# Ternary feed-forward layer: the value half and the product move to VectorE, both rounding passes to ScalarE, and the tile loop is written out

## The reference, cut to what matters

```python
def bit_linear(x, w, b):
    gamma_x = clip(max(abs(x), axis=-1, keepdims=True), 1e-05, None)
    scale_x = 127.0 / gamma_x
    x_dq = clip(round(x * scale_x), -128.0, 127.0) / scale_x
    gamma_w = clip(mean(abs(w)), 1e-05, None)
    w_dq = clip(round(w / gamma_w), -1.0, 1.0) * gamma_w
    return einsum('bsd,hd->bsh', x_dq, w_dq) + b
gate = silu(bit_linear(x, gate_w, gate_b))      # 256 -> 1024
val = bit_linear(x, val_w, val_b)               # 256 -> 1024
return bit_linear(gate * val, out_w, out_b)     # 1024 -> 256, added to x
```

## Time and profile before

| | |
|---|---|
| median of 3 runs | 2538.33 us (2534.33 to 2542.36) |
| the profiled execution's own time | 2534.81 us |
| its span in the profile | 2533.1 us |
| busy: TensorE matmul, VectorE, ScalarE, GpSimd | 1971.6, 1433.2, 1018.5, 822.2 us |
| the stage of the change | first VectorE instruction at 2383.33 us, last at 2529.58 us |
| granted TensorE clock, mean of the execution | 0.884 |

### The profile page before, as it was taken

The page is one execution under the profiler, slowest core; times in us unless marked ns, Lnnn a source line. Parts: engine busy times, 40 slices in busy tenths (PEclk is TensorE's granted clock), DMA queues, the critical chain, the costliest instruction groups (busy, mean ns, idle before and its releaser), DMA issues. The chain is left out here.

```text
span 2533.1 us, 45181 instructions
## 1 busy us (share of the span) xinstructions
PE 1971.6 (78%) x12069; PEld 1342.1 (53%) x12070; DVE 1433.2 (57%) x3465; ACT 1018.5 (40%) x2717; POOL 822.2 (32%) x783
## 2 busy tenths in 40 slices
PE   4999999979998997245599997388755689898355
PEld 3666666655555655123466665255523457676122
DVE  3565666647763335135533443677678517777598
ACT  3454455542222121012244443155477326767233
POOL 1333333320000001661255655122100126655276
PEclk9999999999998898677799999599967889989576
DMA  9940000000000002222487885200010011111000
GB/s 307 283 115 0 0 0 0 0 1 0 0 0 1 0 0 95 102 96 83 111 165 167 174 167 81 67 1 0 0 52 1 4 26 30 35 34 32 22 15 19
DMA packets 143984, 144.79 MB, mean 57 GB/s; under 512 B 49216, under 2 KB 133408, under 8 KB 143136
## 3 DMA queue, kind: packets, MB, share of 16 engines
q1 hardware_dynamic: 120864, 113.81, 15.6%
q0 software_dynamic: 23040, 30.01, 7.1%
HBM read 137.12 MB, written 66.44 MB: 80 GB/s over the span
## 5 line engine op out<-in xcount | busy, mean ns | idle before, releaser
L1406 POOL DMA_INDIRECT expert_sums<-moe_rows_in,moe_to x128 | 197.9, 1546 | 228.3 <-ACT moe_rows_in L1598 133.6
L1492 PE MATMUL moe_gate<-moe_places,moe_xt 128*128 x512 | 175.9, 466 | 2.0 <-issue 1.2
L1681 DVE COPY moe_ht_e<-moe_turned 128x256 f32<-128x256 f32 x128 | 54.3, 424 | 197.9 <-PE moe_turned L1500 171.1
L2723 POOL TENSOR_TENSOR wa_low<-wa_low,wa_top 128x512 f32<-128x512 f32 x128 | 133.1, 1040 | 101.7 <-DVE wa_top L2924 100.8
L251 POOL TENSOR_TENSOR ga_q_inv<-ga_q_sum,half 128x4 f32<-128x4 f32 x64 | 64.4, 1007 | 312.4 <-DVE ga_q_sum L421 312.4
L529 ACT ACTIVATE ga_prob<-ga_score,ga_neg_max 128x128 f32<-128x128 f32 x256 | 99.6, 390 | 153.9 <-DVE ga_neg_max L438 153.9
L2921 DVE SCALAR_TENSOR_TENSOR wa_low<-wa_score,wa_table 128x512 f32<-128x512 f32 x128 | 87.8, 686 | 63.1 <-PE wa_score L2762 60.6
L347 PE MATMUL ga_summed<-ga_wo,ga_out_t 128*128 128x256 f32 x512 | 122.8, 383 | 0.7 <-ACT ga_out_t L537 0.7
L285 PE MATMUL ga_proj<-ga_wq,ga_xt 128*128 128x512 f32 x256 | 122.6, 602 | 0.0
L347 PEld LDWEIGHTS ga_summed<-ga_wo,ga_out_t 128*128 128x128 f32 x512 | 98.1, 192 | 40.6 <-issue 29.2
L1189 POOL DMA_INDIRECT slot_x<-moe_xn,mr_slot_to x96 | 94.5, 985 | 70.4 <-issue 51.9
(11 more groups left out here) (430 smaller groups left out, 5113.2 us busy)
## 6 DMA issues: line engine op xcount, KB each, us to landing
moe_places<-in_L_ffn_packed SPq DMA_DIRECT2D x128, 608.0 KB
slot_x<-zeros SPq DMA_DIRECT2D x24, 1076.0 KB, 16.2
moe_rows_in<-slot_x SPq DMA_DIRECT2D x128, 134.5 KB
mc_rows<-expert_sums SPq DMA_DIRECT2D x8, 512.0 KB, 7.6
wa_v<-v_ctx SPq DMA_DIRECT2D x16, 180.0 KB, 3.0
x<-in_x SPq DMA_DIRECT2D x1, 2048.0 KB, 8.7
ctxt<-in_ctx_t SPq DMA_DIRECT2D x1, 2048.0 KB, 13.2
ga_wq<-in_L_xattn_Wq SPq DMA_DIRECT2D x1, 2048.0 KB, 16.9
```

The costliest lines, as they stand in the source:

```text
L1406: pool.indirect_dma_start(out=mem.sums[j % SUMS], out_offset=bass.IndirectOffsetOnAxis(ap=to[:, j:j + 1], axis=0), in_=y[:, j, :], in_offs ...
L1492: last = pe.matmul(both[j % 2][:, 0:2 * FE], xt[:, j % 2, c, :], packed[:, place, c * 2 * FE:(c + 1) * 2 * FE].rearrange("p a n -> p (a n) ...
L2723: pool.tensor_tensor(unit, unit, top[:, k % LOWS, :].unsqueeze(2).to_broadcast([P, QUAD, P]), ALU.subtract).then_inc(lowered.sem, 1)
```

## The change

Of the tile's work, the value half becomes one VectorE pass per half that reads PSUM, scales and adds the bias (L3186 of the changed kernel, the same form as `pre`). The product becomes a VectorE pass of 1024 columns (L3202), with two SBUF inputs. Both rounding passes become ScalarE `Identity` activations of 1024 columns: `shifted` with `per` as scale and a column of ROUND as bias (L3154), `rounded` with a column of -ROUND as bias (L3157); GpSimd fills the two columns once. ScalarE no longer moves the value banks. GpSimd keeps only the 16 additions of the output bias, issued one after another at the start of the stage. The copy into `xs` is gone; TensorE reads `mem.xnt16` itself. `gate`, `val` and `prod` have one buffer each; `far`, `size`, `per` and `scale_o` have two columns. Gate and value matmuls go gate, gate, value, value by halves with a signal for each half, and run one tile ahead and not two. All 16 tiles are written out, with constants for the tile numbers.

The diff, cut to its core:

```diff
         scale_g, scale_v = sb("scale_g", [P, B]), sb("scale_v", [P, B])
-        xs = sb("xs", [P, 2, HC, P], BF16)
-        pre, shifted = sb("pre", [P, F]), sb("shifted", [P, F])
-        gate, val = sb("gate", [P, 2, F]), sb("val", [P, 2, F])
+        pre, gate, val, prod, shifted = (sb(x, [P, F]) for x in ("pre", "gate", "val", "prod", "shifted"))
         rounded = sb("rounded", [P, F], BF16)
         ht = sb("ht", [P, FC, P], BF16)
...
+        up_by, down_by = sb("up_by", [P, 1]), sb("down_by", [P, 1])
+        far, size, per, scale_o = (sb(x, [P, 2]) for x in ("far", "size", "per", "scale_o"))
         gates = [bank(f"gates{j}") for j in range(2)]
         vals = [bank(f"vals{j}") for j in range(2)]
         turned, down = bank("turned", BF16), bank("down")
...
+        scaled, rounding_set = signal("scaled"), signal("rounding_set")
         biased = signal("biased")
-        multiplied = signal("multiplied", 1, 2)
...
+        gated, valued = signal("gated"), signal("valued")
+        pre_made, val_made, silued, multiplied = signal("pre"), signal("val"), signal("silued"), signal("multiplied")
+        chain, per_made = signal("chain"), signal("per")
+        lifted, rounded_s = signal("lifted"), signal("rounded")
+        turn, moved, downed, added = signal("turn"), signal("moved"), signal("downed"), signal("added")
+        def behind(engine, sig, n):
+            if n >= 0:
+                engine.wait_ge(sig.sem, sig.at(n))
...
         with nc.Block() as block:
             @block.gpsimd
             def _(pool):
...
+                pool.memset(up_by[:, :], ROUND).then_inc(rounding_set.sem, 1)
+                pool.memset(down_by[:, :], -ROUND).then_inc(rounding_set.sem, 1)
                 pool.wait_ge(mem.tf_loaded.sem, 16 * mem.tf_loads)
...
-                        pool.tensor_copy(xs[:, j % 2, :, :], mem.xnt16[:, :, bass.ds(n * P, P)]).then_inc(staged.sem, 1)
...
-                        pool.tensor_tensor(val[:, j % 2, :], val[:, j % 2, :], w.bv[:, :], ALU.add).then_inc(val_biased.sem, 1)
...
-                        pool.tensor_tensor(val[:, j % 2, :], val[:, j % 2, :], gate[:, j % 2, :], ALU.mult).then_inc(prod_made.sem, 1)
...
-                    pool.tensor_tensor(mem.x_tile(n), mem.x_tile(n), w.bo[:, :], ALU.add).then_inc(biased.sem, 1)
...
+                for n in range(B):
+                    pool.tensor_tensor(mem.x[:, n, :], mem.x[:, n, :], w.bo[:, :], ALU.add).then_inc(biased.sem, 1)
...
             @block.tensor
             def _(pe):
...
+                def up(n, out_banks, weight, read, done):
                     for h in range(2):
...
+                        behind(pe, read, 2 * (n - 1) + h)
+                        for c in range(HC):
+                            last = pe.matmul(out_banks[h][:, :], mem.xnt16[:, c, n * P:(n + 1) * P], weight[:, c, h * HALF:(h + 1) * HALF], start=(c == 0), stop=(c == HC - 1))
+                        last.then_inc(done.sem, 1)
+                def turn_product(n):
+                    pe.wait_ge(rounded_s.sem, rounded_s.at(n))
+                    behind(pe, moved, n - 1)
                     for f in range(FC):
                         last = pe.transpose(turned[:, f * P:(f + 1) * P], rounded[:, f * P:(f + 1) * P], mem.ident16[:, :])
                     last.then_inc(turn.sem, 1)
+                def go_down(n):
                     pe.wait_ge(moved.sem, moved.at(n))
...
+                    behind(pe, added, n - 1)
                     for f in range(FC):
                         last = pe.matmul(down[:, 0:H], ht[:, f, :], w.o[:, f, :], start=(f == 0), stop=(f == FC - 1))
                     last.then_inc(downed.sem, 1)
...
+                up(0, gates, w.g, pre_made, gated)
+                up(0, vals, w.v, val_made, valued)
+                for n in range(B):
+                    if n + 1 < B:
+                        up(n + 1, gates, w.g, pre_made, gated)
+                        up(n + 1, vals, w.v, val_made, valued)
+                    turn_product(n)
+                    go_down(n)
...
             @block.scalar
             def _(act):
...
+                def silu(n):
+                    behind(act, multiplied, n - 1)
                     for h in range(2):
-                        act.activation(val[:, j % 2, h * HALF:(h + 1) * HALF], vals[h][:, :], ACT.Copy, scale=scale_v[:, bass.ds(n, 1)]).then_inc(val_moved.sem, 1)
...
-                        act.activation(gate[:, j % 2, h * HALF:(h + 1) * HALF], pre[:, h * HALF:(h + 1) * HALF], ACT.Silu).then_inc(silued.sem, 1)
...
+                        act.wait_ge(pre_made.sem, pre_made.at(2 * n + h))
+                        act.activation(gate[:, h * HALF:(h + 1) * HALF], pre[:, h * HALF:(h + 1) * HALF], ACT.Silu).then_inc(silued.sem, 1)
+                def round_product(n):
+                    act.wait_ge(per_made.sem, per_made.at(n))
+                    act.activation(shifted[:, :], prod[:, :], ACT.Identity, bias=up_by[:, 0:1], scale=per[:, n % 2:n % 2 + 1]).then_inc(lifted.sem, 1)
+                    behind(act, turn, n - 1)
+                    act.wait_ge(lifted.sem, lifted.at(n))
+                    act.activation(rounded[:, :], shifted[:, :], ACT.Identity, bias=down_by[:, 0:1]).then_inc(rounded_s.sem, 1)
+                def move(n):
                     act.wait_ge(turn.sem, turn.at(n))
...
+                    behind(act, downed, n - 1)
                     act.activation(ht[:, :, :].rearrange("p c s -> p (c s)"), turned[:, :], ACT.Copy).then_inc(moved.sem, 1)
...
+                act.wait_ge(rounding_set.sem, 2)
+                silu(0)
+                for n in range(B):
+                    if n >= 1:
+                        move(n - 1)
+                    round_product(n)
+                    if n + 1 < B:
+                        silu(n + 1)
+                move(B - 1)
...
             @block.vector
             def _(dve):
                 dve.wait_ge(mem.tf_loaded.sem, 16 * mem.tf_loads)
...
                 dve.tensor_scalar(scale_g[:, :], mem.x_step[:, :], w.mean_g[:, 0:1], None, ALU.mult).then_inc(scaled.sem, 1)
                 dve.tensor_scalar(scale_v[:, :], mem.x_step[:, :], w.mean_v[:, 0:1], None, ALU.mult).then_inc(scaled.sem, 1)
                 dve.wait_ge(scaled.sem, 2)
...
+                def halves(n, target, banks, scale, bias, made, done, read):
                     for h in range(2):
                         cols = slice(h * HALF, (h + 1) * HALF)
...
+                        dve.wait_ge(made.sem, made.at(2 * n + h))
+                        behind(dve, *read(n, h))
+                        dve.scalar_tensor_tensor(target[:, cols], banks[h][:, :], scale[:, n:n + 1], bias[:, cols], ALU.mult, ALU.add).then_inc(done.sem, 1)
+                def before_silu(n):
+                    halves(n, pre, gates, scale_g, w.bg, gated, pre_made, lambda n, h: (silued, 2 * (n - 1) + h))
+                    halves(n, val, vals, scale_v, w.bv, valued, val_made, lambda n, h: (multiplied, n - 1))
+                def measure(n):
+                    j = slice(n % 2, n % 2 + 1)
                     def step(k, ins):
                         ins.then_inc(chain.sem, 1)
...
-                    step(2, dve.reciprocal(per[:, :], size[:, :]))
...
-                    step(3, dve.tensor_scalar(shifted[:, :], prod, per[:, 0:1], ROUND, ALU.mult, ALU.add))
...
-                    step(4, dve.tensor_scalar(rounded[:, :], shifted[:, :], ROUND, None, ALU.subtract))
+                        dve.wait_ge(chain.sem, chain.at(2 * n + k))
+                    dve.wait_ge(silued.sem, silued.at(2 * n + 1))
+                    dve.wait_ge(val_made.sem, val_made.at(2 * n + 1))
+                    behind(dve, lifted, n - 1)
+                    dve.tensor_tensor(prod[:, :], val[:, :], gate[:, :], ALU.mult).then_inc(multiplied.sem, 1)
+                    dve.wait_ge(multiplied.sem, multiplied.at(n))
+                    step(0, dve.tensor_reduce(far[:, j], prod[:, :], AX.X, ALU.max, apply_absolute_value=True))
+                    behind(dve, added, n - 2)
+                    step(1, dve.tensor_scalar(size[:, j], far[:, j], 1e-5, 1.0 / 127.0, ALU.max, ALU.mult))
+                    dve.reciprocal(per[:, j], size[:, j]).then_inc(per_made.sem, 1)
+                    dve.tensor_scalar(scale_o[:, j], size[:, j], w.mean_o[:, 0:1], None, ALU.mult).then_inc(scaled.sem, 1)
...
                 def finish(n):
...
-                    dve.tensor_scalar(scale_o[:, :], size[:, :], w.mean_o[:, 0:1], None, ALU.mult).then_inc(chain.sem, 1)
...
+                    row = mem.x[:, n, :]
+                    dve.wait_ge(scaled.sem, scaled.at(n + 2))
+                    dve.wait_ge(biased.sem, biased.at(n))
+                    dve.wait_ge(downed.sem, downed.at(n))
+                    dve.scalar_tensor_tensor(row, down[:, 0:H], scale_o[:, n % 2:n % 2 + 1], row, ALU.mult, ALU.add).then_inc(added.sem, 1)
...
                 before_silu(0)
...
+                for n in range(B):
```

(77 more changed lines are left out.)

54 lines of the change are left out of this document (2 added, 52 removed).

## The result

| | before | changed |
|---|---|---|
| median | 2536.33 us (4 runs) | 2503.74 us (2499.36 to 2516.61, 4 runs) |
| the profiled execution's own time | 2534.81 us | 2499.36 us |
| last stage, first VectorE instruction to the end of the last | 146.7 us | 115.9 us |
| start of the last stage | 2383.33 us | 2378.73 us |

The ratio is 0.9877, interval 0.9834 to 0.9919: the change saves about 31 us, and the interval leaves room for 20 to 42. The stage alone is 30.8 us shorter. The two profiled executions are 35.5 apart because the second also happened to enter the stage 4.6 us earlier, in code that is the same in both; medians of this kernel carry such scatter, the stage does not. Two further profiles of the changed kernel gave 116.0 and 115.9 us for the stage.

A forecast was written before the change was run, and what follows sets the result against it. VectorE, waiting for GpSimd, bounds the last stage; after the change start to 2391.1, 15 tiles of 6.7 and a last tile of 7.1 end at 2498.7 us, a 31.4 us gain, forecast 2507 us, range 2496 to 2520.

The forecast's parts named there:

- its two rounding passes mostly wait for GpSimd's instruction: VectorE, last stage before the change: `shifted` and `rounded` take 4.23 us a tile, 1.44 when left alone.
- The closed loop of 6.45 us: From `per` through ScalarE's rounding passes and next Silu pair, VectorE's product, `far` and `size` to next `per`: 6.45 us.
- TensorE's loop of 7.3 us at the lower clock: Next tile's matmuls, then transposes, `ht` wait and down matmuls: 7.3 us; as the bound 2516 us, chance 0.22.
- The pace of 6.7: Time per tile in the changed last stage: 6.7 us, with 6.2 and 7.3 as ends.
- The start, 7.8 us until the first `per`: Last stage, from VectorE's first instruction at 2383.33 to the first `per` at 2391.1 us.
- the 0.5 that I took: Wait of tile 0's VectorE product for GpSimd's bias additions: 0.5 us, nothing later; up to 1.9 by the skill's rule.
- The sum: Last stage: start, 15 tiles of 6.7 and the last tile alone end at 2498.7 us, a gain of 31.4 us.
- the last tile alone: End of the stage: `shifted` and `rounded`, transposes, `ht`, down matmuls and addition of the last tile, 7.1 us.
- VectorE's own sum, 6.2 us,: VectorE's work per tile in the changed last stage, without waits: 6.2 us, a floor.
- the VectorE rival: VectorE itself bounds the last stage, the clock mostly high: 6.25 us a tile, 2500 us, chance 0.13.
- The table reload: Rival: ScalarE reloads its table twice a tile, 1.283 us each, making the kernel slower, 2543 to 2546 us; chance 0.03.
- The loop's registers: Register instructions of the last stage's tile loop disappear; no gain counted beyond gaps already left out.

## Why the prediction was right, step by step

- *The last stage is bound by VectorE, and its two rounding passes mostly wait for GpSimd's instruction.* Shown: with narrow GpSimd passes and nothing else changed both fall to 0.90 us and the stage by 38 us, as much as the two passes lose.
- *The closed loop of 6.45 us.* Measured 6.46. Its links stand in the timeline of the short tile without a gap. It stays when TensorE's matmuls are halved and goes when the Silu is taken out of it, so it is what I named, and neither engine's own load.
- *TensorE's loop of 7.3 us at the lower clock.* Four tiles took 7.31 to 7.32, but not by that loop: that the numbers agree is luck. The sum takes the matmuls, the transposes and the down matmuls of one tile all at the lower level, and no tile of the stage shows that loop closing: in the long tile shown TensorE goes round in 6.35 us. What took 7.3 was the second half of a path of 13.77 us over two tiles, which leaves TensorE for both other engines and which the prediction did not have. Right is that matmuls at 1.2 GHz hold a tile, through TensorE's order; halving them ends it.
- *The pace of 6.7* was a judgement between the two values, and luck has a part in it. The mean is (2487.31 - 2386.30) / 15 = 6.73, ten tiles at 6.45 to 6.48 and five at 7.16 to 7.32, with the granted clock at 0.81 in the middle of the stage against 0.71 before. Nothing in the prediction could give that share of long tiles.
- *The start, 7.8 us until the first `per`.* Measured 7.65. The product of tile 0 took 1.56 us, of tile 1 1.29, so the wait for the bias additions was 0.34 and 0.07, under the 0.5 that I took and well under the 1.9 that full waits would make. The rule that the prediction cites from the Trainium skill, "SBUF — State Buffer", section "SBUF: two separate sides", and the trace agree on the wait. The price was small because an addition lasts 0.72 us here, not 0.95, and because the products began only 0.47 and 0.20 us before the running one ended. GpSimd waited as well: the addition issued during either product took 1.70 us.
- *The sum.* The stage was to take 115.4 us (2383.3 to 2498.7); it took 115.9: the start 7.65 (7.8 taken), 15 tiles 101.0 (100.5), the last tile alone 7.2 (7.1).
- *VectorE's own sum, 6.2 us,* was 0.3 too high. It is 5.9: the three small passes with their gaps take 0.38 us and not 0.55, the four halves 2.63 and not 2.76. That made the VectorE rival 0.3 us a tile too slow and the expectations of two runs too high, by 2 to 4 and by 3 to 7 us. It did not enter the forecast, since that floor lay below the loop either way, but it set the low end of the range, 2496.
- *The table reload* did not happen: one load, after the first `pre`, as the order showed.
- *The loop's registers* were to bring nothing. Written out alone they bring 1.9 us in the stage, which the time cannot show. What they are worth once VectorE no longer waits for GpSimd was not run.

## What to carry to other kernels

Before work is moved off a busy engine, ask how long its instructions take when nobody else runs: here 2.8 of 8.9 us a tile were waits inside VectorE's instructions, which a table of busy time counts as work. After the move, add up closed loops from one tile to the next through the engines' program order, and not only each engine's load: ScalarE and VectorE each had slack, and the loop through both set the pace. Look also for loops that close only after two tiles, as the 13.77 us here: a sum over one tile cannot show them. Opening both took only another order and two more buffers, and was worth another 12 us of the stage.
